# Weight transposes of a chunk in one group, and unread taps and border rows left out, in a deformable and ternary convolution kernel

## The reference

```python
x = x + L0(_gn(x)); x = x + L1(_gn(x))
# L0: deformable 3x3 convolution
om = conv3x3(x, w_off) + b_off              # 27 channels: off_y, off_x, mask (9 taps each)
py, px = base + tap + off_y, base + tap + off_x
sampled = bilinear(x, py, px) * sigmoid(m)  # 4 corners, zero outside the image, for 9 taps
out = einsum('bckhw,ock->bohw', sampled, weight) + bias
out = group_norm(out, 16) * gamma + beta
# L1: ternary convolutions
q = where(w - mean < lo, -1, where(w - mean > hi, 1, 0))   # lo, hi: thirds of the range
out1 = relu(batchnorm(conv3x3(x, q1))); out = relu(out1 + batchnorm(conv3x3(out1, q2)))
```

## Time and profile before

| | |
|---|---|
| median of three runs | 311.93 us (311.05 to 311.96) |
| the profiled execution | 310.99 us, of which the span of instructions 309.2 us |
| TensorE busy | 273.2 us, 88% of the span, 1712 matmuls |
| VectorE busy | 206.3 us, 67% |
| ScalarE busy | 177.0 us, 57% |
| GpSimd busy | 133.6 us, 43% |
| mean granted TensorE clock | 0.978 |

### The profile page before, as it was taken

One profiled execution on the slowest core, in us unless ns is written; L12 is line 12 of the kernel. 1 busy time (PEld: TensorE's weight loads), 2 busy tenths in 40 slices (PEclk: granted clock), 3 DMA queues, 4 the chain that ended last, 5 costly groups with the idle time before them and its releaser, 6 DMA issues.

```text
span 309.2 us, 5008 instructions
## 1 busy us (share of the span) xinstructions
PE 273.2 (88%) x1712; PEld 239.6 (77%) x1712; DVE 206.3 (67%) x426; ACT 177.0 (57%) x334; POOL 133.6 (43%) x189
## 2 busy tenths in 40 slices
PE   2999999799999989998998989998899976999900
PEld 2768787699989889997998889997777755777700
DVE  3798666688998899759878788785253625006184
ACT  2549654688866968977789777882043006321052
POOL 8350376376666858777657966503000000000031
PEclk9999999999999999999999999999999997999985
DMA  7900966844333332333323333200000000000006
GB/s 248 330 3 3 302 202 183 271 126 136 116 114 106 113 88 77 103 107 108 108 64 106 104 103 111 83 0 2 0 0 2 0 0 0 0 2 0 2 36 243
DMA packets 25031, 28.60 MB, mean 93 GB/s; under 512 B 2461, under 2 KB 22541, under 8 KB 25000
## 3 DMA queue, kind: packets, MB, share of 16 engines
q1 hardware_dynamic: 24496, 26.98, 27.2%
q10 hardware_dynamic: 504, 1.24, 1.2%
HBM read 19.87 MB, written 6.78 MB: 86 GB/s over the span
## 4 chain that ended last, share of the span: by engine, by line
PE 71%; DVE 16%; ACT 8%; issue 2%; DMA 1%; ACTq 0%
PE PS L683 23%; PE PS L571 10%; PE PS L534 9%; PE PS L607 5%; PE PS L589 4%; PE PS L608 4%; PE PS L609 4%; PE PS L591 4%; PE PS L590 4%; DVE slo L1179 3%; DVE st L1081 2%; ACT vhi L847 2%; DVE vlo L1186 2%; ACT shi L840 2%; DVE xb L1279 2%
## 5 line engine op out<-in xcount | busy, mean ns | idle before, releaser
L453 POOL TENSOR_TENSOR vt<-rowm,hat 128x1026 f32<-128x1026 f32 x36 | 70.8, 1968 | 37.5 <-PE PS L571 36.8
L1179 DVE TENSOR_TENSOR slo<-PS,shi 114x512 fp32r<-114x512 f32 x72 | 53.6, 751 | 12.8 <-ACT shi L840 12.6
L1186 DVE TENSOR_TENSOR vlo<-PS,vhi 128x576 fp32r<-128x576 f32 (+2 forms) x84 | 50.3, 619 | 13.0 <-ACT vhi L847 13.0
L840 ACT ACTIVATE shi<-PS 114x512 fp32r<-114x512 f32 x72 | 46.3, 652 | 20.0 <-PE PS L571 19.7
L571 PE MATMUL PS<-ident,vt 128*114 128x128 f32 x324 | 47.4, 275 | 1.4 <-DVE nsm L1032 0.7
L847 ACT ACTIVATE vhi<-PS 128x576 fp32r<-128x576 f32 (+2 forms) x84 | 44.0, 546 | 7.4 <-PE PS L591 5.1
L589 PE MATMUL PS<-shi,patch 114*128 114x288 f32 x136 | 43.8, 322 | 1.9 <-DVE omh L1329 1.5
L607 PE MATMUL PS<-vhi,wdhi 128*128 128x256 f32 x144 | 43.0, 299 | 2.1 <-ACT xb L854 2.0
L683 PE MATMUL PS<-xhi,q 128*128 128x512 f32 x144 | 39.6, 422 | 4.2 <-ACT xhi L915 4.2
L473 POOL TENSOR_TENSOR xb<-xb,xs 128x512 f32<-128x512 f32 x3 | 3.7, 1274 | 87.3 <-ACT xb L920 87.3
L591 PE MATMUL PS<-shi,patch 114*128 114x288 f32 x136 | 40.8, 300 | 0.0
(11 more groups left out here) (146 smaller groups left out, 438.4 us busy)
## 6 DMA issues: line engine op xcount, KB each, us to landing
patch<-xt SPq DMA_DIRECT2D x136, 114.0 KB
xt<-xtt SPq DMA_DIRECT2D x4, 1024.0 KB, 7.1
xs<-in_x SPq DMA_DIRECT2D x3, 512.0 KB, 7.4
out<-xb SPq DMA_DIRECT2D x6, 256.0 KB, 2.3
wraw<-in_L_conv_w SPq DMA_DIRECT2D x2, 576.0 KB, 9.0
omr<-omr SPq DMA_DIRECT2D x8, 128.0 KB, 4.2
wd_raw<-in_L_conv_weight ACTq DMA_DIRECT2D x1, 576.0 KB, 6.5
xs<-in_x SPq DMA_DIRECT2D x2, 256.0 KB, 4.2
```

The source lines that it names most:

```text
L453: g.tensor_tensor(vt[:, n % 2, :, :].rearrange("p t (r j) -> p t r j", r=WR), rowm[:, n % 2, :, :].unsqueeze(3).to_broadcast([P, TAPS, WR, ...
L840: a.activation(shi[:, n % 2, lo:hi], S_PS[:, lo:hi], ACT.Copy).then_inc(shi_ok, 1)
L1179: d.tensor_tensor(slo[:, n % 2, lo:hi], S_PS[:, lo:hi], shi[:, n % 2, lo:hi], ALU.subtract).then_inc(slo_ok, 1)
L1186: last = d.tensor_tensor(places(vlo), src, places(vhi), ALU.subtract)
```

## The change

The nine transposes of a chunk stand in one group behind the second piece of combining. One copy and one split follow, of 9 x 128 columns at once. `s_mm`, `shi_ok` and `slo_ok` count one for each chunk. The wait for `slo_ok` ahead of `beside(n)` and the second piece stays at its place. The last chunk of an image (one pair) transposes six taps and 64 pixels, and copies only these. Pairs 0 and 16 of an image are sampled only for the taps that are read (6 of 9). The convolutions leave out the border row of zeros, 15 rows for 16 in three of nine matmuls; the centre tap, which covers all rows, goes first in the high part and last in the low part.

```diff
+        def taps_at(n, u):
+            s = 4 * (n % CH) + 2 * u
+            return (K, TAPS) if s == 0 else (0, 2 * K) if s == H else (0, TAPS)
+
+        def weights_at(m, n):
+            v = m.rearrange("k (t p) -> k t p", p=P)
+            return v if pairs(n) == 2 else v[:, 0:2 * K, 0:P // 2]
...
+            if s == 0:
+                parts = ((0, 3, 9, 0), (1, 3, 9, 1))
...
+        TAP_ORDER = [[K + 1] + [k for k in range(TAPS) if k != K + 1], [k for k in range(TAPS) if k != K + 1] + [K + 1]]
+
+        def tap_rows(h, k):
+            return (1 if (h, k // K) == (0, 0) else 0), H // 2 - (1 if (h, k // K) == (1, K - 1) else 0)
+
+        def tap_out(m, h, k):
+            r0, r1 = tap_rows(h, k)
+            return square(m)[:, r0:r1, :]
+
+        def tap_in(img, b, h, k):
+            r0, r1 = tap_rows(h, k)
+            r = b % RING * ROWS + h * (H // 2) + k // K
+            return img[:, r + r0:r + r1, k % K:k % K + W]
...
-                    pool.wait_ge(s_mm, 2 * n - 2)
+                    pool.wait_ge(s_mm, n - 1)
...
-                for k in range(TAPS):
-                    r = b % RING * ROWS + h * (H // 2) + k // K
-                    last = t.matmul(OFF_PS[(2 * b + h) % 4], woffT[:, k, :], (xhi, xlo)[part][:, r:r + H // 2, k % K:k % K + W],
-                                    start=(k == 0 and part == 0), stop=(k == TAPS - 1 and part == 1))
+                for i, k in enumerate(TAP_ORDER[part]):
+                    last = t.matmul(tap_out(OFF_PS[(2 * b + h) % 4], h, k), woffT[:, k, :], tap_in((xhi, xlo)[part], b, h, k),
+                                    start=(i == 0 and part == 0), stop=(i == TAPS - 1 and part == 1))
...
-            def turn_weights_out(n, part):
+            def turn_weights_out(n):
                 pe.wait_ge(vt_ok, n + 1)
                 if n:
-                    pe.wait_ge(slo_ok, 2 * n - 1 + part)
+                    pe.wait_ge(slo_ok, n)
...
-                for tap in range(*PARTS[part]):
-                    last = t.transpose(S_PS[:, tap * P:(tap + 1) * P], vt[:, n % 2, tap, :], ident[:, :])
+                m = P if pairs(n) == 2 else P // 2
+                for tap in range(taps_at(n, pairs(n) - 1)[1]):
+                    last = t.transpose(S_PS[:, tap * P:tap * P + m], vt[0:m, n % 2, tap, :], ident[0:m, 0:m])
                 last.then_inc(s_mm, 1)
...
+                t0, t1 = taps_at(n, u)
                 for e in range(2):
                     m = 2 * u + e
-                    at = (slice(None), slice(2 * u, 2 * u + 2), slice(None), slice(e * HALF, (e + 1) * HALF))
-                    t.matmul(V_PS[u][:, e, :], patch[:, n % PATCHES, m, 0, :], hi[at], start=True, stop=False)
+                    at = (slice(None), slice(2 * u, 2 * u + 2), slice(t0, t1), slice(e * HALF, (e + 1) * HALF))
+                    v = V_PS[u][:, e, :].rearrange("c (q t w) -> c q t w", q=2, t=TAPS)[:, :, t0:t1, :]
+                    t.matmul(v, patch[:, n % PATCHES, m, 0, :], hi[at], start=True, stop=False)
...
                 if n >= 0 and n + 1 < CHUNKS:
-                    pe.wait_ge(slo_ok, 2 * n + 4)
+                    pe.wait_ge(slo_ok, n + 2)
                     used = beside(n)
-                if n + 2 < CHUNKS:
-                    turn_weights_out(n + 2, 0)
                 if piece_at(n, 1):
                     combine(*piece_at(n, 1))
                 if n + 2 < CHUNKS:
                     if used:
                         pe.wait_ge(*used)
-                    turn_weights_out(n + 2, 1)
+                    turn_weights_out(n + 2)
...
-                lo, hi = (P * tap for tap in PARTS[part])
-                a.activation(shi[:, n % 2, lo:hi], S_PS[:, lo:hi], ACT.Copy).then_inc(shi_ok, 1)
+                a.activation(weights_at(shi[:, n % 2, :], n), weights_at(S_PS[:, 0:TAPS * P], n),
+                             ACT.Copy).then_inc(shi_ok, 1)
...
-                lo, hi = (P * tap for tap in PARTS[part])
-                d.tensor_tensor(slo[:, n % 2, lo:hi], S_PS[:, lo:hi], shi[:, n % 2, lo:hi], ALU.subtract).then_inc(slo_ok, 1)
+                d.tensor_tensor(weights_at(slo[:, n % 2, :], n), weights_at(S_PS[:, 0:TAPS * P], n),
+                                weights_at(shi[:, n % 2, :], n), ALU.subtract).then_inc(slo_ok, 1)
```

More of the change, by code:

```diff
@@ L279, in v_parts @@
             s = 4 * (n % CH) + 2 * u
-            if s == 16:
+            if s == 0:
+                parts = ((0, 3, 9, 0), (1, 3, 9, 1))
+            elif s == 16:
                 parts = ((0, 0, 6, 16), (0, 6, 9, 0), (1, 0, 3, 17), (1, 3, 9, 1))
@@ L290, in v_parts @@
                     for q, t0, t1, slot in parts]
-        PARTS = ((0, 4), (4, TAPS))
+        TAP_ORDER = [[K + 1] + [k for k in range(TAPS) if k != K + 1], [k for k in range(TAPS) if k != K + 1] + [K + 1]]
[8 more added lines that the diff above has]
+            return img[:, r + r0:r + r1, k % K:k % K + W]
         PIECES = ((8, 7), (6, 5, 4), (3, 2), (1, 0))
@@ L531, in offset_part @@
                     pe.wait_ge(off_sum, 2 * b + h - 3)
-                for k in range(TAPS):
-                    r = b % RING * ROWS + h * (H // 2) + k // K
-                    last = t.matmul(OFF_PS[(2 * b + h) % 4], woffT[:, k, :], (xhi, xlo)[part][:, r:r + H // 2, k % K:k % K + W],
-                                    start=(k == 0 and part == 0), stop=(k == TAPS - 1 and part == 1))
+                for i, k in enumerate(TAP_ORDER[part]):
+                    last = t.matmul(tap_out(OFF_PS[(2 * b + h) % 4], h, k), woffT[:, k, :], tap_in((xhi, xlo)[part], b, h, k),
+                                    start=(i == 0 and part == 0), stop=(i == TAPS - 1 and part == 1))
                     for sums, n, at in SUMS.get((b, h, part), ()):
-                        if k == at:
+                        if i == at:
                             sums(GN0, n)
@@ L577, in sample @@
                     return
-                pe.wait_ge(slo_ok, 2 * n + 2)
+                pe.wait_ge(slo_ok, n + 1)
                 pe.wait_ge(patch_in[n % PATCHES], patches_through(n))
@@ L585, in sample @@
                 hi, lo = (m[:, n % 2, :].rearrange("k (t q w) -> k q t w", t=TAPS, q=4) for m in (shi, slo))
+                t0, t1 = taps_at(n, u)
                 for e in range(2):
                     m = 2 * u + e
-                    at = (slice(None), slice(2 * u, 2 * u + 2), slice(None), slice(e * HALF, (e + 1) * HALF))
-                    t.matmul(V_PS[u][:, e, :], patch[:, n % PATCHES, m, 0, :], hi[at], start=True, stop=False)
-                    t.matmul(V_PS[u][:, e, :], patch[:, n % PATCHES, m, 0, :], lo[at], start=False, stop=False)
-                    last = t.matmul(V_PS[u][:, e, :], patch[:, n % PATCHES, m, 1, :], hi[at], start=False, stop=True)
+                    at = (slice(None), slice(2 * u, 2 * u + 2), slice(t0, t1), slice(e * HALF, (e + 1) * HALF))
+                    v = V_PS[u][:, e, :].rearrange("c (q t w) -> c q t w", q=2, t=TAPS)[:, :, t0:t1, :]
+                    t.matmul(v, patch[:, n % PATCHES, m, 0, :], hi[at], start=True, stop=False)
+                    t.matmul(v, patch[:, n % PATCHES, m, 0, :], lo[at], start=False, stop=False)
+                    last = t.matmul(v, patch[:, n % PATCHES, m, 1, :], hi[at], start=False, stop=True)
                 last.then_inc(v_mm, 1)
@@ L680, in conv_part @@
                 pe.wait_ge(ready, B + b + 1 if done is c1_mm else 2 * b + h + 1 + (h == 0))
[L681 to L684, removed]
+                for i, k in enumerate(TAP_ORDER[part]):
+                    last = t.matmul(tap_out(PS[:, 2 * b + h, :], h, k), q[:, k, :], tap_in(src, b, h, k),
+                                    start=(i == 0 and part == 0), stop=(i == TAPS - 1 and part == 1))
                 if part:
@@ L726, in _ @@
                 t.matmul(O_PS, wdhi[:, 0, :], vhi[:, 0:WROWS, TAPS - 1, :], start=False, stop=True).then_inc(o_mm, 1)
-                pe.wait_ge(shi_ok, 2 * SPECULATED + 4)
+                pe.wait_ge(shi_ok, SPECULATED + 2)
                 pe.wait_ge(vt_ok, SPECULATED + 4)
@@ L731, in _ @@
                 pe.sem_inc(v_mm, B * PAIRS - pairs_through(SPECULATED - 1))
-                pe.sem_inc(s_mm, 2 * (CHUNKS - SPECULATED - 2))
+                pe.sem_inc(s_mm, CHUNKS - SPECULATED - 2)
                 for b in range(B):
@@ L833, in hats, with weights_hi @@
                 a.activation(v, v, ACT.Relu, scale=-1.0, bias=1.0).then_inc(hat_ok, 1)
-            def weights_hi(n, part):
-                act.wait_ge(s_mm, 2 * n + part + 1)
+            def weights_hi(n):
+                act.wait_ge(s_mm, n + 1)
                 if n >= 2:
                     act.wait_ge(v_mm, pairs_through(n - 2))
-                lo, hi = (P * tap for tap in PARTS[part])
-                a.activation(shi[:, n % 2, lo:hi], S_PS[:, lo:hi], ACT.Copy).then_inc(shi_ok, 1)
+                a.activation(weights_at(shi[:, n % 2, :], n), weights_at(S_PS[:, 0:TAPS * P], n),
+                             ACT.Copy).then_inc(shi_ok, 1)
```

(18 more changed lines are left out.)

## The result

Median of five runs 332.99 us (332.48 to 337.28) against 311.87 (310.96 to 311.96); ratio 1.071, 95% interval 1.066 to 1.076 (the two medians alone give 1.068). The forecast was 329, range 315 to 335.

What follows compares the result with a forecast made beforehand. TensorE was taken to bound the ordinary slot. The profiled 310.99 us plus 20.3 for the 36-slot loop less 1.9 for the convolutions gave 329.4, taken as 329; range 315 to 335, the forecast case's own 322 to 334.

Steps and rivals of the forecast that it cites:

- the ring: In a slot TensorE waits for the split, combines (0.72 us) and runs nine transposes (0.91): at least 4.50 us.
- the sum up to it: From a slot's first sampling matmul (T), copy and split run serially; the wait is met at T+2.86, before T+1.89.
- plain slots: Seven loop slots with three taps: 4.50 us, or 4.93 with ternary transposes; together +0.9 us.
- the combine behind the wait: Six matmuls after TensorE's wait for the split: 0.72 us, 0.79 less 0.08 for the first matmul after a transpose.
- output slot: Slot ending an output row group: combine waits for ScalarE's output copies, about T+3.2, slot 4.83 us; five together +1.2.
- The main term: Twelve loop slots ending on a small reduction: later statistics and transposes behind the wait, +14.2 us, bounds 3.3 to 16.7.
- Rival (B): VectorE makes up the late split in the twelve reduction slots, costing 3.3 us instead of 14.2: 318.5 us; chance 0.20.
- Rival (D): More TensorE standing drops its clock from 2.4 to 1.2 GHz in the loop, three 1.7 us dips: 334.5 us; chance 0.07.
- The signs: Expected in the profile: copy 1.14 us, split 1.36, longer TensorE waits, ordinary slots 4.5 and 4.8, loop near 176.
- Rival (C): Copy and split together under 2.07 us, or an early copy, so the savings count, some 6 us: 305 us; chance 0.09.
- border sampling matmul: Sampling at image borders, 48 matmuls of 192 columns instead of 288: 46 ns saved each, 2.2 us of TensorE in all.
- the prediction's case of 0.11 each: Last chunk's 24 small transposes: if weight loads set the pace, each stays at 0.11 us, sum 1.2 us higher.

Runs made afterwards that it cites:

- e3: Changed kernel with its one group of nine transposes, but semaphore counts after four and nine, and copy and split in two parts; 316.27 us, ratio 1.012.
- e10: Changed kernel with transposes in two groups (four ahead of the second combining piece, five behind), still one copy and one split; 329.69 us, ratio 1.055.
- e5: Changed kernel with the first matmul of the second sampling issued three more times in slots with no three-tap piece; 334.20 us, ratio 1.074.
- e4: Kernel before with only the border rows left out of the three convolutions; 309.98 us, ratio 0.994.
- e1: Changed kernel with transposes, copies and splits in two parts again, unread taps and border rows still left out; 308.43 us, ratio 0.989.
- e6: Kernel before with only unread taps left out of sampling, transposes, copies and splits, convolutions whole; 310.66 us, ratio 0.996.
- e9: As e1, but both transpose groups ahead of the second combining piece where beside(n) has no work; 306.15 us, ratio 0.981.

## Why the prediction was right, and where it was off

**The durations and the ring.** Copy 1134 ns for 1.14 us, split 1358 for 1.36, the smaller copy 491 for 0.49. The split ends at T+2.80, as the sum up to it says, and what waits for it starts at T+2.86 (slots 11, 17 and 27), as forecast. Slot 12's transposes start 0.68 us later than before, and the forecast's 1.1 for that slot less its 0.44 gives 0.66. The plain slots 3, 27 and 32 took 4.57 to 4.59 us for 4.50, the three with ternary transposes 5.00 to 5.17 for 4.93, and slot 5 4.84 for 4.50. The step that was too small is the combine behind the wait. The forecast took 0.08 off it, because the first matmul after a transpose takes extra; after a stand it takes extra too (0.22 us to the next one for 0.12, slot 27). In slot 27 the combine takes 0.82 us for the 0.72 (from 199.27 to 200.09), the transposes 0.90 for 0.91. Slot 4, an output slot, took 5.07 for 4.83, with the output at T+3.35 for 3.2 and the combine at 0.79. The order of waits held, and at full clock no slot was more than 0.5 us off.

**The main term.** Twelve slots with a reduction: +14.2 forecast, +15.5 in the profile. That is closer than it should be. The six of them whose clock stayed at full (8, 9, 21, 22, 30, 31) had +7.1 forecast and took +6.3; the other six had +7.1 forecast and took +9.3, with 10.2 us at half clock among them. e3 (+4.8) and e10 (+10.9) show both halves of the term, the four transposes that went behind the wait and the late split. Rival (B), which had VectorE make this up and gave +3.3 for all twelve, is ruled out by the six at full clock alone.

**Rival (D) in the profile.** The forecast put the clock as another case, and in the profile it came on top. The clock fell to 1.2 GHz five times in the loop, 20.5 us in all, once across slots 24 and 25 for 6.8 us. Without slot 35, the 25 slots at full clock had +11.4 forecast and took +12.2; the ten with some half clock had +9.0 forecast and took +15.0. So the profiled loop missed by 6 us where the clock fell and by 0.8 elsewhere, and in those 25 slots the reductions, forecast 0.8 to 0.9 too high, made up for half of the rest, forecast 1.6 too low. That part is luck. Two other rows price the half clock. The profiled execution has a mean clock of 0.941 over 335.5 us, 39.6 us at half; the other four 0.964 to 0.970, 20 to 24 us; it is 3.5 to 4.8 us longer, so 0.22 to 0.25 us for each us at half clock. And e5's loop is 3.1 us shorter than the changed kernel's with 13.7 us less at half, 0.23. By that the 20.5 us cost some 5, and the profiled loop without them would be some +22.

**Too low by 3 us in the median.** The sum was +18.4 (20.3 less 1.9), and the median rose by 21.1. The clock is not the main reason here. The profile has 19.1 us at half outside the loop; if the other four executions had as much there, only 1 to 5 of their 20 to 24 us fell in the loop, worth 1 us at most. (They have no trace.) Some 2 us are the slots' own (+22 for +20.3), the combine behind a stand and the output slots above all.

**The signs.** Met: one copy and one split of the forecast length, TensorE standing for the split, plain slots near 4.5, the stands for nsm and tw ahead of the transposes (3.6 us in the loop, 0.7 before), and the dips of (D). Not met: the loop took 183 us for about 176, for the reason above, and the second ternary convolution 36.88 us for under 36.3. The border rows did save there, 36.21 us in e4; but in the changed kernel 5.0 us of that stretch were at half clock, and in e4 and the kernel before 3.4. The kernels with two groups and the low weights no later than T+1.85 (before, e1, e4, e6, e9) have no dip in the loop, all others do. That standing of TensorE lowers the clock fits this, but is not shown.

**Rival (C)** needed copy and split under 2.07 us together; they took 2.49. It counted 6 us for the savings, and e1, which has all but the grouping, gained 3.2. Two of its terms were too large. A border sampling matmul was to save 46 ns; in the trace of e1 these step at 112 ns where 288 columns step at 136, so 24 ns were saved, 1.2 us in all for 2.2. The fewer and smaller transposes of an image's last chunk were to save up to 2.5; in e6 the slots that turn it (6, 15, 24, 33) are 0.4 us shorter together. The border rows of the convolutions were right: a matmul of 480 columns steps at 229 ns for 243, so 42 ns for the three of a group for 46, and e4 measured 1.7 us for 1.9.

**The half-height transposes** step at 56 ns for the 0.06 I took (the full ones at 109), all but the first of a group, when the clock is at full. By the Trainium skill ("TensorE: Matmul & The Clock Gate", section "Step-by-step: what each phase is for") a weight load takes time by its columns and not by its rows. The small transposes load 114 columns as the full ones do; their step shows that such a load holds up a series for no more than 56 ns, so it didn't set the pace of 109, and the prediction's case of 0.11 each is out.

## What to carry to other kernels

This kernel has a chain over one buffer: transpose, copy, split. With each step in two parts, the next engine starts on the first part while the second is made. Fusing the parts saved 0.15 us an engine in a slot, and made the last result 0.95 us later, because that overlap was gone. Read what waits behind that result before merging, small reductions and output copies above all, and ask of each wait what filled it. The same fact turned round is a gain: independent work (nine transposes) put ahead of a wait took another 2.3 us off the median (e9 against e1, 0.977 to 0.984 against 0.987 to 0.992).

## What the runs showed that I had not expected

A sampling matmul of 192 columns steps at 112 ns, one of 256 at 119, one of 288 at 136 and one of 512 at 243. From 512 to 256 columns the step falls by 0.48 ns a column, and from 256 to 192 by 0.11; what sets it there no run tells, though the 128-column weight loads that go with each are the same. And TensorE's clock fell four times for 3.4 us and once for 6.8 in a loop in which TensorE was busy 83 to 92% of each stretch of 24 to 42 us and stood for 1.8 us at the longest. Two stretches of the kernel after:

```profile
93.00:131.00 38.00, 31.41 (x228) 29.18 (x228) 26.24 (x53) 23.13 (x45) 22.05 (x28) 0.96 0.25 81
...
171.00:213.00 42.00, 36.04 (x247) 34.06 (x247) 24.80 (x47) 25.22 (x47) 24.14 (x32) 0.88 0.25 74
```

(stretch, us, then busy time of PE, PEld, DVE, ACT and POOL, the clock, the DMA share and GB/s.) The first is 83% busy with a clock of 0.96, the second 86% with 0.88; the kernel before had 97% and 94% there and 1.00. In the first of these stretches e10 was 84% busy with 1.00, and e3 from 131 to 171 us 91% with 0.96.
